# Cross-attention: the reads of the next context are begun by ScalarE's queue, no longer by SP's

## The reference

```
x = layernorm(x + self_attention(x))
x = layernorm(x + cross_attention(x, ctx))
x = layernorm(x + ffn(x))
```

```
Q = text @ Wq + bq ; K = features @ Wk + bk          # features = ctx[b], 375 x 1024
scores = Q @ K^T / sqrt(1024) ; attn = softmax(scores)
attended = attn @ features
```

## Time and profile before

| what | value |
|---|---|
| median of 3 runs | 1948.36 us (1944.59 to 1948.92) |
| the profiled execution | 1946.6 us, its span 1944.9 us |
| mean granted clock of TensorE | 0.989 |
| TensorE busy | 1824.9 us, 94% |
| VectorE / ScalarE / GpSimd busy | 887.3 / 430.2 / 350.6 us |
| instructions | 26655 |

### The profile page before, as it was taken

How to read it: one execution, slowest core, us unless ns; L and a number is a source line. 1 busy time by engine, 2 the same in 40 slices (tenths; PEclk the granted TensorE clock), 3 DMA queues, 4 the chain that set the end, 5 groups by cost and what they waited for, 6 DMA issues and landing times.

```text
span 1944.9 us, 26655 instructions
## 1 busy us (share of the span) xinstructions
PE 1824.9 (94%) x10214; PEld 1023.1 (53%) x10214; DVE 887.3 (46%) x1342; ACT 430.2 (22%) x660; POOL 350.6 (18%) x261
## 2 busy tenths in 40 slices
PE   4898899888888969999999999999999999999998
PEld 2666644577767734444445444444545444444443
DVE  5688641668878864443443444344343311111111
ACT  3222110444444422222222222222222200000000
POOL 0222377212222211121111112111111000000000
PEclk9999999999999979999999999999999999999999
DMA  9242761479999953112111211212121321221220
GB/s 309 76 143 77 190 192 43 96 167 236 235 236 251 219 100 65 44 34 59 35 44 38 56 44 34 59 35 44 37 54 40 116 102 53 102 102 69 85 102 22
DMA packets 300527, 196.67 MB, mean 101 GB/s; under 512 B 260024, under 2 KB 274552, under 8 KB 298300
## 3 DMA queue, kind: packets, MB, share of 16 engines
q1 hardware_dynamic: 294236, 192.85, 39.2%
q10 hardware_dynamic: 6240, 3.15, 0.6%
HBM read 105.30 MB, written 50.80 MB: 80 GB/s over the span
## 4 chain that ended last, share of the span: by engine, by line
PE 51%; issue 32%; DVE 8%; POOL 4%; DMA 3%; ACT 1%; SPq 1%; POOLq 0%; DVEq 0%; ACTq 0%
PE psum L1276 49%; POOL arena L1016 2%; DMA arena<-in_x 2%; POOL small L942 1%; DVE arena L715 1%; PE psum L1485 1%; POOL arena L951 1%; DMA arena<-in_L_xattn_Wq 1%; DMA x_parts_scratch<-arena 1%; PE psum L1503 1%; PE psum L1269 1%; DVE arena L830 1%; DVE arena L495 1%; DVE small L684 0%; DVE small L410 0%
## 5 line engine op out<-in xcount | busy, mean ns | idle before, releaser
L1276 PE MATMUL psum<-arena 128*128 128x448 f16 (+9 forms) x9432 | 1753.0, 347 | 60.2 <-POOL arena L1016 15.7
L1276 PEld LDWEIGHTS psum<-arena 128*128 128x128 f16 (+5 forms) x9432 | 973.8, 106 | 820.5 <-issue 104.6
L1040 POOL TENSOR_TENSOR arena<-arena 128x1024 f16<-128x1024 f32 (+1 forms) x65 | 138.3, 2128 | 692.7 <-ACT arena L1218 692.7
L883 DVE SCALAR_TENSOR_TENSOR arena<-psum,small,arena 128x448 f32<-128x448 f32 x84 | 57.4, 684 | 409.0 <-PE psum L1276 409.0
L924 DVE SCALAR_TENSOR_TENSOR arena<-psum,small,arena 128x512 f32<-128x512 f32 x28 | 21.0, 750 | 333.1 <-PE psum L1276 320.9
L942 POOL TENSOR_TENSOR small<-small 112x1 f32<-112x1 f32 (+1 forms) x46 | 37.0, 804 | 588.5 <-DVE small L384 588.4
L1218 ACT ACTIVATE arena<-arena 128x1024 f16<-128x1024 f32 (+1 forms) x65 | 68.7, 1057 | 277.8 <-DVE arena L869 277.8
L1231 ACT ACTIVATE arena<-arena 128x448 f16<-128x448 f32 (+1 forms) x88 | 50.7, 576 | 291.9 <-DVE arena L883 291.9
L1016 POOL TENSOR_TENSOR arena<-arena 128x224 f16<-128x224 f32 x64 | 62.0, 969 | 144.4 <-ACT arena L1137 144.4
L889 DVE TENSOR_TENSOR arena<-arena 128x448 f16<-128x448 f32 (+1 forms) x88 | 55.0, 625 | 57.5 <-ACT arena L1231 57.5
L867 DVE TENSOR_TENSOR arena<-arena,psum 128x1024 f32<-128x1024 uint32 x65 | 79.4, 1221 | 2.6
(11 more groups left out here) (179 smaller groups left out, 750.0 us busy)
## 6 DMA issues: line engine op xcount, KB each, us to landing
h_scratch<-arena SPq DMA_DIRECT2D x88, 224.0 KB, 2.9
arena<-h_scratch SPq DMA_DIRECT2D x13, 1408.0 KB, 6.1
arena<-in_ctx SPq DMA_DIRECT2D x32, 512.0 KB, 4.5
arena<-in_x SPq DMA_DIRECT2D x32, 448.0 KB, 5.7
x_scratch<-arena SPq DMA_DIRECT2D x32, 448.0 KB, 3.5
arena<-in_L_ffn_down_qweight SPq DMA_DIRECT2D x21, 512.0 KB
x_parts_scratch<-arena SPq DMA_DIRECT2D x16, 448.0 KB, 5.5
arena<-in_ctx SPq DMA_DIRECT2D x16, 448.0 KB
```

Of the source, the lines that this page charges most:

```text
L883: dve.scalar_tensor_tensor(h_f[0:n, :], up[0:n, :], sc_u[0:n, :], g_act[0:n, :], ALU.mult, ALU.mult).then_inc(s_hf, 1)
L1040: pool.tensor_tensor(dst[1], src, dst[0], ALU.subtract).then_inc(s_wl, 1)
L1276: mm = pe.matmul(out, a, r, start=(k == 0), stop=(k == len(pairs) - 1))
```

## The change

The reads of the context of batch n+3 leave SP's program and enter ScalarE's, behind its last high part of the context of n+2. Chunks, waits and semaphores are the same. It happens for the batches n = 0 to 12; the reads of the contexts 0, 1 and 2 stay with SP. No computation is changed.

```diff
+            ctx_rows = ctx_d.rearrange("b s d -> (b s) d")
+
+            def next_ctx(n):
+
+                for c in range(CC):
+                    base = n * CTX + c * P
+                    act.wait_ge(s_cl, CC * (n - 1) + c + 1)
+                    if c < CC - 1:
+                        act.dma_start(cx[:, c, :], ctx_rows[bass.ds(base, P), :]).then_inc(s_cx[c], 16)
+                        continue
+                    even = CP[c] // 16 * 16
+                    act.dma_start(cx[0:even, c, :], ctx_rows[bass.ds(base, even), :]).then_inc(s_cx[c], 16)
+                    act.dma_start(cx[even:CP[c], c, :], ctx_rows[bass.ds(base + even, CP[c] - even), :]).then_inc(s_cx[c], 16)
...
                     if has(2):
                         context_hi(n + 2, (b + 2) % GB, 2)
+                    if has(3):
+                        next_ctx(n + 3)
...
                         sp.wait_ge(s_y3, 2 * (n + 1))
                         load_residual(n + 2, (b + 2) % GB)
-                    if loop or n + 3 < NB:
-                        next_ctx(n + 3)
```

## The result

The changed kernel takes 1973.95 us (median of 4 runs, 1968.56 to 1990.28) against 1946.47 us in the same runs of the kernel before (1940.3 to 1948.92). The ratio is 1.0152, 95% interval 1.0124 to 1.0181: slower by 1.5%, where 1942.4 us was forecast. The profiled execution took 1969.41 us, its span 1967.7 us, clock 0.982.

A forecast was written before the change was run, and what follows sets the result against it. It took cross-attention to be held by TensorE's and VectorE's waits for SP's queue. Terms: -6.5 us on SP, +0.5 on ScalarE, so 1946.6 became 1940.6, as a median 1942.4 us; range 1936 to 1957.

The forecast's parts named there:

- The ceiling of 10.4 us: Cross-attention: most that could be gained by removing TensorE's and VectorE's waits for SP's queue, 10.3 to 10.5 us.
- the 39.6 worked out: Cross-attention: predicted time in us of a pair of batches without those waits, from the last full pair, corrected for clock.
- SP's part: SP's queue: x1 transposes start 5.1 us earlier, context transposes and store up to 5.1 us; gain 6.5 us.
- the middle: Midway between best and worst, SP's context transposes end 2.35 us earlier; the gain was taken as 6.5 us.
- the one called disputed: Whether the DMA engines can carry SP's transposes 5.1 us earlier while context reads pass through the same engines.
- best: Transposes and reads at their own rates: 13.9 us, ending 4.7 us earlier, winning the full 10.4 us.
- worst: The same 4.49 MB at 242 GB/s takes 18.5 us; the end stays and nothing is won.
- The third: Rival: context reads land after 7.7 us, VectorE's line 684 waits 13 times, +16.5 - 6.5 us, median 1958; chance 0.08.
- no change: First rival: the DMA engines are the wall, only the beginning is won, median 1947.4 us; chance 0.25.
- The second rival: ScalarE held in its own read issues, 2.84 us each, delaying its exponential 13 times; median 1986 us; chance 0.13.

The follow-up runs named there:

- the kernel with little data: Changed kernel, but ScalarE's context reads fetch only the first 64 of 1024 columns, with the same issues and waits (also called the small-read kernel): 1933.95 us, ratio 0.9922.
- the order of issue held: Changed kernel, but SP waits behind each batch's residual until ScalarE has issued the context reads: 1960.59 us, ratio 1.0065.

## Why the prediction was wrong

**The bound.** Right in kind: the waits for SP's queue were real, and a better order in one queue took 8.8 us off. The ceiling of 10.4 us was low: the kernel with little data ran 14.7 us faster than before (1933.95 against 1948.68), and its pairs of 39.1 us are shorter than the 39.6 worked out.

**SP's part.** Right. The x1 transposes started 0.25 us behind the residual's issue, and in one queue the same order gave -8.8 us (1948.68 to 1939.90) where -6.5 was forecast. That this is so near is partly luck: the triple there ended only 1.5 us sooner (18.2 us in place of 19.7), less than the 2.35 counted for the middle, so the sum does not explain the whole gain.

**The step that failed** is the one called disputed: what the DMA engines carry when the reads come from another queue. I bounded it by "best", both kinds at their own rates side by side (13.9 us for the 4.49 MB), and "worst", the 242 GB/s of the whole pair, in which "nothing is won". Neither end held. The triple that was to end 4.7 us earlier, or at worst at the same time, ended 2.7 us later (22.4 us after the residual's start in place of 19.7). 242 GB/s is the rate of transfers that are begun from one queue; no row of the trace before has transposes and reads from two queues at once. In flight together they moved 107 and 121 GB/s. A bound taken from one way of sharing isn't a bound for another, and the range "from both sides" needed an end below nothing there.

**The rivals.** The third, "the reads land late", was the one that came true, with a chance of 0.08. Its sign and place were right: line 684 waited 12 times, 27.9 us, where 13 times and 16.5 us were counted. Its size, 1958 us, was short for two reasons beside the clock. The reads landed up to 15.1 us after their issue (7.7 was taken, midway between 4.1 and 11.2), and it left out that the transposes would slow down with them, to a triple of 14.79 us; so the gain of 6.5 us that it kept was partly gone as well. The 11.2 us landing of the earlier trace rows was a warning of that size, though beside a plain copy and not beside transposes, and the weight given to it was too small. The rule of the Trainium skill that is cited there ("DMA: Bandwidth & Descriptors", "Queues, rings and completion order"), that an engine takes turns between queues a packet at a time, is not contradicted: in 541 to 546.5 us of the changed kernel SP's queue moved 0.25 MB and ScalarE's 0.34 MB, so both went on, only slowly. The other rule, of the Trainium skill's section "Issuing engines are not separate DMA queues" on the same page, that transfers of all issuers run on the same engines and a second issuer saves only issuing time, would have given no change. The two plain queues at 406 to 422 GB/s fit it; with transposes in one of them the result was 1.5% slower, and there the measurement decides.

**Held issues.** The second rival was wrong. ScalarE's issues took 0.33 to 0.37 us in the median, less than the 0.58 counted, and the small-read kernel, which has them all and is faster than before, shows no cost of them.

**What the prediction left out of every price** is the clock; it used it only to correct one pair. Of the 25 us in five pairs, TensorE's busy time is 194.1 us against 181.4 before, 12.7 us for the same matmuls; the rest is idle time. Two rows of TensorE in the changed kernel:

```profile
499.34 6.29 PE L1292 MATMUL psum<-arena 128*112 128x512 f16 x18 [6.46 <-DVE arena L721]
...
520.76 4.09 PE L1292 MATMUL psum<-arena 128*112 128x512 f16 x18 [1.34 <-DVE arena L721]
```

The same 18 matmuls took 6.29 us after 6.46 us of idling and 4.09 after 1.34. The granted clock was 0.64 in the first stretch and 1.00 in the second, so most of the first ran at the lower of the two levels, 1.2 GHz, and not 2.4. In these five pairs the added idle time was thus charged about twice: 12.4 us as idle time and 12.7 us in slower matmuls. The length of the last wait alone doesn't decide it: the kernel before ran at 1.00 behind 2.87 us of idling.

## What to carry to other kernels

Before a transfer is moved to another issuing queue, ask what it will be in flight with: beside DMA transposes of the other queue, plain reads and the transposes both slowed down here (8.0 us added for 2.7 us worth of bytes), and the busy share of the engines doesn't show it; only bytes per second do. When a queue's order holds something back, first try another order in the same queue: here the x1 transposes ahead of the reads, all on SP, take 0.47% off (0.9953, 0.9936 to 0.997) where the second queue added 1.5%. And where no row shows a kind of sharing, leave room on the losing side.

## What the hardware showed that was not expected

- Two queues, transposes in one and reads in the other: 121 GB/s over 8 us with nothing else in flight, against 210 for transposes alone and 387 for reads. Two queues of plain reads: 406 to 422 GB/s. The queue tables of the profile say where the time is: a transpose packet took 67 ns of an engine in the mixture (90.7% of 16 engines over 8 us for 1726 packets) and 22 ns alone (113.4% over 5 us for 4155), a read packet 291 ns (33.0% for 145) and 152 ns alone (100.9% over 2.7 us for 287). So the engines aren't idle in between; each packet takes longer. Why is shown by no run here. Transposes on ScalarE's queue with the reads on SP's weren't tried.
- A DMA busy share above 1 means little: 1.24 went with 121 GB/s, 1.25 with 285.
- The collapse isn't in every overlap: with the order of issue held, five triples that each followed the last read of the other queue by some 0.5 us took 14.90, 8.36, 13.21, 10.66 and 8.01 us. What decides it in a given batch stays open.
